# Attention scores in a graph network: the query and key weights multiplied with each other once, at the start

## The reference

```python
h = jnp.maximum(_layernorm(x, axis=-1), 0.0)          # 6250 x 128
x = x + L1(h, edge_index, edge_attr_10, Wq, bq, Wk, bk, Wv, bv, We, Wskip, bskip, gamma, beta)

# inside L1, with d = 128
q_all = x @ Wq.T + bq
k_all = x @ Wk.T + bk
e = edge_attr @ We.T                                   # 10 attributes an edge
q = q_all[dst]
k = k_all[src] + e
alpha = (q * k).sum(-1) / jnp.sqrt(d)                  # one score an edge
# softmax over the edges of one destination, weighted sum of v_all[src] + e
```

## Time and profile before

| | |
|---|---|
| Median of 3 runs | 6253.74 us (6252.82 to 6256.91) |
| The profiled execution's own time | 6284.8 us |
| Its span in the trace | 6283.2 us |
| TensorE matmul, busy | 5208.7 us (83%) |
| TensorE weight load, busy | 3811.9 us (61%) |
| VectorE, busy | 3834.3 us (61%) |
| ScalarE, busy | 2610.9 us (42%) |
| GpSimd, busy | 2402.3 us (38%) |

### The profile page before, as it was taken

How to read it: one execution, slowest core, us unless ns; L and a number is a source line. 1 busy time by engine, 2 the same in 40 slices (tenths; PEclk the granted TensorE clock), 3 DMA queues, 4 the chain that set the end, 5 groups by cost and what they waited for, 6 DMA issues and landing times.

```text
span 6283.2 us, 112603 instructions
## 1 busy us (share of the span) xinstructions
PE 5208.7 (83%) x41944; PEld 3811.9 (61%) x41944; DVE 3834.3 (61%) x6063; ACT 2610.9 (42%) x4935; POOL 2402.3 (38%) x2152
## 2 busy tenths in 40 slices
PE   1199999668888777788778777599999999969997
PEld 0166666436666666666666666266666666636665
DVE  4688888557666666666666665466666666530001
ACT  0066666444444444444444444344444444300001
POOL 3212210047777777777777776000000000001110
PEclk6599999889999999999999999799999999969998
DMA  6246656257666666666677676233333333226664
GB/s 174 68 170 217 208 194 198 100 156 199 188 193 193 196 193 184 189 190 194 191 194 195 186 194 192 92 139 132 128 128 138 139 129 128 85 88 207 206 203 128
DMA packets 797185, 1040.87 MB, mean 166 GB/s; under 512 B 464063, under 2 KB 683700, under 8 KB 769572
## 3 DMA queue, kind: packets, MB, share of 16 engines
q1 hardware_dynamic: 706421, 881.14, 42.5%
q0 software_dynamic: 87488, 151.98, 10.7%
q10 hardware_dynamic: 2738, 0.54, 0.0%
HBM read 635.06 MB, written 411.01 MB: 166 GB/s over the span
## 4 chain that ended last, share of the span: by engine, by line
PE 48%; POOL 30%; issue 9%; DVE 7%; DMA 4%; SPq 1%; ACT 1%; DVEq 0%; POOLq 0%; ACTq 0%
PE psum L1367 40%; POOL G L822 14%; POOL H L822 14%; PE psum L1639 7%; DVE R L845 3%; DVE H L845 1%; DMA H<-gather_table,cols_pc 1%; DMA G<-gather_table,cols_pc 1%; POOL R L778 1%; DVE lns L851 1%; POOL ACC L771 1%; SPq L546 1%; ACT HT L1699 1%; PE psum L1485 1%; PE psum L1607 0%
## 5 line engine op out<-in xcount | busy, mean ns | idle before, releaser
L1699 ACT ACTIVATE R<-psum 128x512 f32<-128x512 f32 (+2 forms) x1452 | 841.0, 580 | 1143.2 <-PE psum L1607 623.9
L822 POOL DMA_INDIRECT G<-gather_table,cols_pc x908 | 1013.2, 1116 | 425.8 <-issue 271.7
L1367 PE MATMUL psum<-R,HT 128*128 128x384 bf16 x6076 | 1085.0, 326 | 59.8 <-DVEq L1356 59.8
L1367 PE MATMUL psum<-R,l 128*128 128x512 f32 (+2 forms) x2375 | 1114.2, 537 | 18.4 <-DMA l<-gather_table,nidx 10.1
L822 POOL DMA_INDIRECT H<-gather_table,cols_pc x896 | 1012.6, 1130 | 273.3 <-issue 268.7
L1367 PE MATMUL psum<-R 128*128 128x98 bf16 (+3 forms) x6858 | 975.0, 280 | 77.7 <-DVE R L845 56.5
L845 DVE TENSOR_TENSOR HT<-HT,psum 128x512 f32<-128x512 f32 (+1 forms) x949 | 622.1, 656 | 461.0 <-PE psum L1367 450.7
L1699 ACT ACTIVATE H<-psum 128x512 f32<-128x512 f32 (+1 forms) x752 | 420.4, 559 | 1020.1 <-PE psum L1587 743.0
L845 DVE TENSOR_TENSOR ACC<-ACC 128x1568 bf16<-128x1568 bf16 x896 | 830.2, 968 | 0.0
L1367 PEld LDWEIGHTS psum<-R,HT 128*128 128x128 bf16 x6076 | 566.9, 97 | 383.9 <-DVEq L1356 60.1
L807 POOL DMA_DIRECT2D node_sums<-G x148 | 131.8, 890 | 1535.3 <-ACT G L1699 1473.8
(11 more groups left out here) (233 smaller groups left out, 7053.4 us busy)
## 6 DMA issues: line engine op xcount, KB each, us to landing
weighted_blocks<-X SPq DMA_DIRECT2D x179, 784.0 KB
adjacency_blocks<-HT SPq DMA_DIRECT2D x74, 1568.0 KB, 5.8
ACC<-weighted_blocks SPq DMA_DIRECT2D x28, 3136.0 KB, 10.4
R<-weighted_blocks SPq DMA_DIRECT2D x28, 3136.0 KB, 10.4
HT<-adjacency_blocks SPq DMA_DIRECT2D x50, 1568.0 KB, 6.5
H<-local_dst_pairs SPq DMA_DIRECT2D x113, 512.0 KB
R<-attr_parts SPq DMA_DIRECT2D x451, 99.0 KB
R<-adjacency_blocks SPq DMA_DIRECT2D x24, 1568.0 KB, 6.5
```

Of the source, the lines that this page charges most:

```text
L822: pool.indirect_dma_start(out=slot(p)[:, 0:F], out_offset=None, in_=table, in_offset=edge).then_inc(s_g[p // GR % 8], 16)
L1367: return nc.tensor.matmul(o, lhs_t, rhs, start=start, stop=stop)
L1699: return nc.scalar.activation(o, a, f, **kw)
```

## The change

At the start, the kernel now multiplies the weights with each other: one product gives Wqᵀ times (Wk, bk, We), 128 x 139, which ScalarE scales by -1/sqrt(128) and writes over `C`. Two small ones give the constant parts (Wkᵀ bq, and bkᵀ bq with Weᵀ bq), which go to `cols[:, 7:8]` and the new `xbias`. Later the turned queries come straight from `HT`: step 2 above is gone, step 3 reads `HT` in place of `QT` and adds the constants as it leaves PSUM. `WT` loses Wq; the counts of later product stages go down by one.

```diff
-        WT = sb("WT", [P, 4, P])
+        WT = sb("WT", [P, 3, P])
+        xbias = sb("xbias", [X1, 1])
...
                 v.wait_ge(s_qh, 2 * b + 1)
-                tt(rest, psum[0:X1, 6 + b % 2, 0:n * P], QX3[:, 0, at], ALU.subtract).then_inc(s_qx, 1)
+                v.scalar_tensor_tensor(rest, psum[0:X1, 6 + b % 2, 0:n * P], xbias[:, 0:1], QX3[:, 0, at],
+                                       ALU.add, ALU.subtract).then_inc(s_qx, 1)
...
-            for k, m in enumerate((1, 2, 3, 4)):
+            for k, m in enumerate((2, 3, 4)):
                 nc.tensor.transpose(bank4(6)[:, k, :], Wm[:, m, :], ident[:, :])
+
+            mm(psum[:, 4, 0:FX], Wm[:, 1, :], C[:, :])
+            mm(psum[:, 4, FX:FX + 1], C[:, 0:F], cols[:, 3:4])
+            mm(psum[0:X1, 4, FX + 1:FX + 2], C[:, F:FX], cols[:, 3:4])
...
             t.wait_ge(s_trc, 2 * NB)
-            products(1, lambda bank, w, n: mm(psum[:, bank, 0:n * P], WT[:, 0, :], HT[:, w * P:(w + n) * P]))
-            t.wait_ge(s_moc, 2 * NB)
             for b, (w0_, n) in enumerate(BLK):
...
-                mm(psum[:, 4 + b % 2, 0:n * P], C[:, 0:F], QT[:, w0_ * P:(w0_ + n) * P])
-                mm(psum[0:X1, 6 + b % 2, 0:n * P], C[:, F:FX], QT[:, w0_ * P:(w0_ + n) * P]).then_inc(s_q, 1)
+                mm(psum[:, 4 + b % 2, 0:n * P], C[:, 0:F], HT[:, w0_ * P:(w0_ + n) * P])
+                mm(psum[0:X1, 6 + b % 2, 0:n * P], C[:, F:FX], HT[:, w0_ * P:(w0_ + n) * P]).then_inc(s_q, 1)
...
-            activation(cols[:, 7:8], cols[:, 3:4], ACT.Copy, scale=-SCALE)
+            activation(C[:, :], psum[:, 4, 0:FX], ACT.Copy, scale=-SCALE)
+            activation(cols[:, 7:8], psum[:, 4, FX:FX + 1], ACT.Copy, scale=-SCALE)
+            activation(xbias[:, :], psum[0:X1, 4, FX + 1:FX + 2], ACT.Copy, scale=-SCALE)
...
-            use_products(1, QT, ACT.Identity, cols[:, 7:8], -SCALE)
             for b, (w0_, n) in enumerate(BLK):
                 act.wait_ge(s_q, b + 1)
-                activation(QX3[:, 0, w0_ * P:(w0_ + n) * P], psum[0:X1, 6 + b % 2, 0:n * P], ACT.Copy).then_inc(s_qh, 1)
-                activation(QT[:, w0_ * P:(w0_ + n) * P], psum[:, 4 + b % 2, 0:n * P], ACT.Copy).then_inc(s_qh, 1)
+                activation(QX3[:, 0, w0_ * P:(w0_ + n) * P], psum[0:X1, 6 + b % 2, 0:n * P], ACT.Identity,
+                           bias=xbias[:, 0:1]).then_inc(s_qh, 1)
+                activation(QT[:, w0_ * P:(w0_ + n) * P], psum[:, 4 + b % 2, 0:n * P], ACT.Identity,
+                           bias=cols[:, 7:8]).then_inc(s_qh, 1)
```

More of the change, by code:

```diff
@@ L706, in _ @@
             load_block(0)
-            sp.wait_ge(s_mo, 3 * NB)
+            sp.wait_ge(s_mo, 2 * NB)
             load_block(1)
@@ L723, in _ @@
             sp.dma_start(ACC[:, :, 0:F], agg_d[1][0:W * P, :].rearrange("(w p) f -> p w f", p=P)).then_inc(s_sum, 16)
-            sp.wait_ge(s_moc, 5 * NB)
+            sp.wait_ge(s_moc, 4 * NB)
             sp.dma_start(out[0:FULL * P, :].rearrange("(w p) f -> p w f", p=P), X[:, 0:FULL, :]).then_inc(s_out, 16)
@@ L1313, in _ @@
             v.wait_ge(s_agn, NB)
-            batch_norm(1, 2, cols[:, 5:6], cols[:, 6:7])
+            batch_norm(1, 1, cols[:, 5:6], cols[:, 6:7])
             layer_norm(2)
@@ L1346, in add_blocks @@
                 v.wait_ge(s_moc, (use + 1) * NB)
-            add_blocks(3)
+            add_blocks(2)
             layer_norm(3)
@@ L1360, in _ @@
             v.sem_inc(s_z, 1)
-            add_blocks(4)
+            add_blocks(3)
         @block.tensor
@@ L1617, in attention_out @@
                 o = psum[:, bank, 0:n * P]
-                mm(o, WT[:, 1, :], AGT[:, nodes], stop=False)
+                mm(o, WT[:, 0, :], AGT[:, nodes], stop=False)
                 mm(o, VXT[:, :], EXT[:, nodes], start=False, stop=False)
-                return mm(o, WT[:, 2, :], HT[:, nodes], start=False)
-            products(2, attention_out)
+                return mm(o, WT[:, 1, :], HT[:, nodes], start=False)
+            products(1, attention_out)
             transposes_back(1)
@@ L1663, in scattered_out @@
                     o = bank4(bank)[:, j, :]
-                    mm(o, HT[:, (w + j) * P:(w + j + 1) * P], WT[:, 3, :], stop=False)
+                    mm(o, HT[:, (w + j) * P:(w + j + 1) * P], WT[:, 2, :], stop=False)
                     ins = mm(o, ones[0:1, :], b2row[:, :], start=False)
                 return ins
-            products(3, scattered_out)
+            products(2, scattered_out)
             t.wait_ge(s_hsplit, 2)
@@ L1691, in plain_out @@
                 return ins
-            products(4, plain_out)
+            products(3, plain_out)
         @block.scalar
@@ L1713, in _ @@
             act.wait_ge(s_wt, 1)
-            activation(cols[:, 7:8], cols[:, 3:4], ACT.Copy, scale=-SCALE)
+            activation(C[:, :], psum[:, 4, 0:FX], ACT.Copy, scale=-SCALE)
+            activation(cols[:, 7:8], psum[:, 4, FX:FX + 1], ACT.Copy, scale=-SCALE)
+            activation(xbias[:, :], psum[0:X1, 4, FX + 1:FX + 2], ACT.Copy, scale=-SCALE)
             activation(VXT[:, :], psum[0:X1, 5, 0:P], ACT.Copy)
-            activation(WT[:, :, :], bank4(6), ACT.Copy).then_inc(s_wtc, 1)
+            activation(WT[:, :, :], bank4(6)[:, 0:3, :], ACT.Copy).then_inc(s_wtc, 1)
             def layer_norm(l):
@@ L1789, in sum_products @@
                                accum_out=bsum[:, b:b + 1]).then_inc(s_moc, 1)
-            def use_products(use, o, func, bias, scale=1.0):
-                for b, (w0_, n) in enumerate(BLK):
-                    act.wait_ge(s_mo, use * NB + b + 1)
-                    activation(o[:, w0_ * P:(w0_ + n) * P], psum[:, 2 + b % 2, 0:n * P], func, bias=bias, scale=scale).then_inc(s_moc, 1)
             def batch_norm(l, func, scratch):
@@ L1862, in _ @@
             copy_blocks(3, EXT, rows=X1)
-            sum_products(2, HT, ACT.Relu, cols[:, 4:5])
+            sum_products(1, HT, ACT.Relu, cols[:, 4:5])
             batch_norm(1, ACT.Identity, AGT)
```

## The result

The changed kernel takes a median of **6243.29 us** (6230.89 to 6258.94, 20 runs), the kernel before in the same comparison 6254.44 us (6238.91 to 6267.92, 20 runs). The ratio is 0.9983, with a 95% interval of 0.9975 to 0.9991: 11 us less, 0.17%, with 6 to 16 us by the interval. Forecast were 6241.4 us and 12.3 us less. The interval leaves out 1, so there is a gain; it is smaller than the 0.2% that the prediction took as the least that can be told from no change.

The account below looks back on a forecast made before the run. No single engine bounds the whole; the chain through the query stage and TensorE's turned loop sets the barrier before the gathers. -12.53 + 0.24 = -12.3 us, so 6253.74 - 12.3 = 6241.4 us, range 6235 to 6249.

Parts of the forecast that it names:

- The stage, 12.53 us: Removed query products, from their first to the first turned product, drain included: 12.53 us off the chain.
- It is worth what it takes: Turned products can start at 1286.68 us instead of 1299.21, and everything behind the barrier moves with them.
- the whole gain was hidden: Rival: attention bound by something the barrier does not start; time 6250 to 6254 us; chance 5%.
- The period of 2.01 us: Turned-query loop: TensorE still sets 2.01 us a block, so the 13 blocks cost what they did.
- The margin: Turned-query loop: VectorE's steps become 1.90 us against the 2.01 us period, leaving 0.11 us, at most 0.04 at the upper bound.
- The tail, +0.24 us: After TensorE's last turned product: one bias (0.12) and two longer subtracts (2 x 0.06) show, between +0.12 and +0.4 us.
- The sum's bounds: Range given for the total of -12.3 us: -11.9 to -12.6 us.
- The start and the stores, nothing: Weight products at the start (at most 2.7 us, some 6 us of cover) and earlier query stores cost nothing.
- The clock: Rival: turned products run at clock 0.50, at most 2.01 us more a block, 6268 us; chance 2%.
- the scatter behind the barrier: Attention's gathers: same pattern, only earlier, with ±4 us allowed because three earlier runs lay within 4.1 us.
- the attention longer by more than 5 us: Sign that the prediction is wrong: the attention behind the barrier takes over 5 us more.
- within 4 us of the 2574.6: Sign of being right: first to last gather stays within 4 us of 2574.6 us (1328.5 to 3903.1).

Follow-up runs that it names:

- early loads: Early gathers, with SyncE's six row and attribute loads issued ahead of the queries' stores: ratio 0.9961 on the second chip, 0.9954 on the third.
- early gathers: Changed kernel, with VectorE clearing sums and setting ones ahead of the turned-query loop, then releasing GpSimd's gathers: 6235.05 us, ratio 0.9964; third chip 0.9968.

## Why the prediction was right

- **The stage, 12.53 us**: measured 12.56 on the chain (1299.21 to 1286.65), 12.55 with the stage alone taken out, 12.53 to 12.54 for each that was put back.
- **It is worth what it takes**: five kernels set the shift of the barrier beside the mean difference of time. -12.3 gave -10.8 ± 4.7, -12.9 gave -11.1 ± 5.3, -12.6 gave -6.9 ± 6.0, -0.2 gave +0.1 ± 5.4, and +39.0 gave +41.3 ± 6.4. All agree with one for one. The last shows it, since it alone is far above its error; the first two exclude that the whole gain was hidden, and not that a few us of it were. That the median came within 1.9 us of the forecast is in part luck: 20 runs of each kernel place the difference to 5 us.
- **The period of 2.01 us**: unchanged, TensorE busy throughout, and the first product began 0.05 us behind the last copy into `HT` (1286.60 to 1286.65). The margin was real, at about 0.18 us instead of 0.11, since a subtract starts before the step ahead of it has ended: 0.45 us more on VectorE, and the period became 2.27.
- **The tail, +0.24 us**: measured +0.21 (29.30 to 29.51). Two sizes in it: the subtract +0.062 as taken (678 to 740 ns), the bias +0.091 rather than 0.117. The rows of 687 and 570 ns differ in more than the bias: each of the 687 waits for a semaphore of its own, and none of the 570 does. The trace of the kernel before has a pair that both wait (groups by shape, whole span):

```profile
L1699 ACT ACTIVATE HT<-psum 128x512 f32<-128x512 f32 x36 | 21.2, 598 | 51.3 <-PE psum L1485 50.9
...
L1699 ACT ACTIVATE HT<-psum,cols 128x512 f32<-128x512 f32 x24 | 16.5, 688 | 30.9 <-PE psum L1367 30.4
```

That is 90 ns for the bias, and 28 ns (570 to 598) for an activation that waits itself. The 24 have no immediate scale and the row of 687 has one, so the scale cost nothing here. The page that I had set against the row was the better source: the Trainium skill, "ScalarE: Activation LUTs", section "What ACT_TABLE_LOAD costs", gives about 93 ns for a pointer operand, and the trace agrees with 91 and 92.

- **The sum's bounds** were added up wrongly: +0.12 and +0.4 on -12.53 give -12.4 to -12.1, not -12.6 to -11.9. The measured -12.35 lies in both.
- **The start and the stores, nothing**: `WT` was 0.72 us later where 2.7 was the bound, and the first store was issued at 1290.10 us (forecast 1289.9). Both stayed covered.
- **The clock**: 1.00 in the loop. That rival did not occur.
- **The step that was mis-sized** is the scatter behind the barrier. I gave ±4 us, from three runs that lay within 4.1 us, and named as a sign of error "the attention longer by more than 5 us", and of being right "within 4 us of the 2574.6". The 20 runs of the same kernel spread over 29 us, with a standard deviation of 7 to 8, so ±4 us for one execution was too narrow. The attention's length met neither sign: it was 36 us shorter, and the medians moved by 11 all the same. Even by that spread 36 us is more than two executions should differ by; the 2574.6 us had been read from an execution slower than all 45 others. Three executions are too few to say how much an execution scatters, and a criterion on one profile's length was worth nothing here.

Not settled: whether the attention as a whole answers to the change by one or two us. No comparison here can show that. Nor is it shown why one execution has more long gathers than another; beside what the long ones stand is told in the last section.

## What to carry to other kernels

A stage that lies on the chain ahead of a barrier, while the engine behind the barrier idles, was worth its length here, and the length is to be read from start to start of what follows, drain included. Before the difference of two profiled executions is explained, it is to be set against the scatter of the runs: from the stretch's first product to the first gather each kernel repeated to 0.1 us, while behind the barrier one kernel's executions differ by 10 us and more, and only the first can be read from one profile. And where such a barrier joins several resources (cleared buffers, queries, attributes), it pays to ask for each engine which one it needs: giving GpSimd its own signal brought about as much again as the whole change (8 to 13 us), until a load that stood late in the queue stopped it.

## What the runs showed of the hardware

One program takes 6254 to 6257 us on one chip and 6540 to 6566 us on two others. Ahead of the attention they agree: the kernel before has its first gather at 1328.51 and 1329.18 us. In the attention it is 2821 to 2854 us from the first gather to the last in the eight profiles of the second and third chip, and 2538 to 2575 in the six of the first. The waits of TensorE in that stretch, by engine and tile (idle us, times, longest), of the kernel before on the second chip:

```profile
PEld psum L1367 <- issue: 727.0, 726, 9.1
...
PE psum L1367 <- issue: 369.0, 390, 8.9
```

And on the first chip, where the row for the matmuls does not occur at all:

```profile
PEld psum L1367 <- issue: 9.9, 5, 6.8
```

So TensorE stands still some 370 us there, up to 9 us at a time, with nothing that the profile shows to wait for; on the third chip it is 423.5 us in the changed kernel with the start's product eight times. What it waits for is open; no experiment here touched it. On the third chip, too, gathers that run during the loop stretched the loop, and on the first they did not: TensorE's first turn came at 1327.51 and 1315.18 us. On the second it stretched as well, with gathers and early loads together. In the profiles of these two chips without early gathers it kept its length, the run with the extra cast aside.

The long gathers stand beside VectorE's work. Four lines of the changed kernel's timeline:

```profile
1325.19 0.94 POOL L823 DMA_INDIRECT G<-gather_table,cols_pc  x1 [0.30 <-issue]
...
1326.16 1.23 DVE L846 TENSOR_TENSOR R<-ACC 128x2048 bf16<-128x2048 bf16 x1 [5.13 <-DMA ACC<-pair_columns]
...
1326.44 1.76 POOL L823 DMA_INDIRECT G<-gather_table,cols_pc  x1 [0.30 <-issue]
...
1328.50 0.94 POOL L823 DMA_INDIRECT G<-gather_table,cols_pc  x1 [0.30 <-issue]
```

Counted over the whole trace of the kernel before: 634 of its 1804 gathers took over 1000 ns, and 633 of them overlap in time a VectorE operation (on two tensors, on a tensor and a scalar, or a cast) that reads SBUF and not PSUM. Of the 1170 shorter ones 450 do. The 721 that overlap none took 943 to 1009 ns. In the changed kernel it is 615 of 616, and on the second chip, of the kernel before, 490 of 491. What all gathers together took above the median of those beside no VectorE work (947 ns before, 944 changed) is 317 us in the kernel before and 287 in the changed one: 30 of the 36 us lie there, and the rest in the 3 ns. This is what stands side by side in the traces; no run took VectorE's operations away from the gathers, so that they cause it is not tested.

A gain of a tenth of a per cent is comparable between chips only as a ratio to a kernel run beside it: the changed kernel's was 0.9983 on both on which it ran.
